# Four-bit rounding of a Perceiver block: the rounding constant made from |q| by ScalarE and a maximum by GpSimd, in place of an exponent mask on VectorE

## The reference

```
scale = max(max|xb| / 6, 1e-12)            per block of 16
q     = nearest of {0, .5, 1, 1.5, 2, 3, 4, 6} to |xb / scale|, with its sign
out   = q * scale
gate  = fq(x) @ fq(w_gate).T ;  up = fq(x) @ fq(w_up).T
y     = fq(silu(gate) * up) @ fq(w_down).T
```

## Time and profile before

| | us |
|---|---|
| median of 3 runs | 1688.79 (1688.48 to 1689.01) |
| the profiled execution, its own time | 1689.68 |
| its span in the profile | 1687.9 |
| attention stage with weight rounding | 211.8 to 347.2 |
| FP4 stage | 348.4 to 520.4 |

### The profile page before, as it was taken

The page is one execution under the profiler, slowest core; times in us unless marked ns, Lnnn a source line. Parts: engine busy times, 40 slices in busy tenths (PEclk is TensorE's granted clock), DMA queues, the critical chain, the costliest instruction groups (busy, mean ns, idle before and its releaser), DMA issues. The chain is left out here.

```text
span 1687.9 us, 26535 instructions
## 1 busy us (share of the span) xinstructions
PE 1471.6 (87%) x11120; PEld 1060.0 (63%) x11120; DVE 773.1 (46%) x1333; ACT 466.4 (28%) x772; POOL 557.9 (33%) x315
## 2 busy tenths in 40 slices
PE   8788977477988999999999999999998896936796
PEld 3556755243444778778787787788776673415573
DVE  2455279989435341332322323222232315978913
ACT  0323301031111115243242433324243431303302
POOL 6102057656323032122122122231232324617701
PEclk9779975788998999999999999999999998967997
DMA  5300030010101411111111111111012016003000
GB/s 233 149 1 1 0 137 1 0 69 0 75 0 64 147 51 57 52 34 53 39 42 51 39 48 42 38 52 57 30 42 78 22 57 256 0 0 119 1 0 25
DMA packets 50101, 91.29 MB, mean 54 GB/s; under 512 B 28600, under 2 KB 41664, under 8 KB 46912
## 3 DMA queue, kind: packets, MB, share of 16 engines
q1 hardware_dynamic: 49984, 89.60, 15.1%
HBM read 79.89 MB, written 9.70 MB: 53 GB/s over the span
## 5 line engine op out<-in xcount | busy, mean ns | idle before, releaser
L1074 POOL TENSOR_TENSOR ctx_hi<-ctx_raw,one 128x1536 fp32r<-128x1536 f32 (+1 forms) x36 | 102.9, 2858 | 617.5 <-DMA ctx_raw<-in_ctx 426.0
L1328 DVE TENSOR_TENSOR V<-PS,vbias 128x512 f32<-128x512 f32 (+1 forms) x104 | 71.9, 691 | 338.0 <-PE PS L1114 337.8
L1256 ACT COPY ET<-PS 128x512 f32<-128x512 f32 (+1 forms) x224 | 129.6, 585 | 299.1 <-PE PS L1170 295.4
L1359 DVE TENSOR_SCALAR_CACHE_REDUCE E<-PS 128x384 f32<-128x384 f32 (+1 forms) x256 | 131.8, 571 | 159.6 <-PE PS L1147 159.0
L1170 PE MATMUL PS<-ident,E 128*128 128x128 f32 (+1 forms) x832 | 127.3, 278 | 8.8 <-ACT ET L1256 8.8
L1077 POOL TENSOR_TENSOR ctx_raw_r<-ctx_raw,ctx_hi 128x1536 fp32r<-128x1536 f32 (+1 forms) x36 | 131.2, 3644 | 2.8
L1114 PE MATMUL PS<-ctx_raw_r,wk_hi 128*128 128x384 f32 (+1 forms) x512 | 128.6, 355 | 0.0
L1114 PE MATMUL PS<-wv_lo,ctx_hi 128*128 128x512 f32 (+1 forms) x416 | 125.9, 405 | 0.0
L1114 PE MATMUL PS<-ctx_hi,wk_hi 128*128 128x384 f32 (+1 forms) x512 | 122.9, 361 | 2.5 <-POOL ctx_raw_r L1077 2.5
L1263 ACT ACTIVATE E<-E,peak 128x1601 f32<-128x1601 f32 x64 | 103.5, 1623 | 64.8 <-DVE peak L1364 64.8
L1114 PE MATMUL PS<-wv_hi,ctx_hi 128*128 128x512 f32 (+1 forms) x416 | 120.5, 411 | 0.8 <-issue 0.8
(11 more groups left out here) (283 smaller groups left out, 2383.3 us busy)
## 6 DMA issues: line engine op xcount, KB each, us to landing
ctx_raw<-in_ctx SPq DMA_DIRECT2D x27, 768.0 KB, 4.4
ctx_raw<-in_ctx_first SPq DMA_DIRECT2D x9, 900.0 KB, 4.6
rel_scr<-rel_out SPq DMA_DIRECT2D x8, 640.0 KB, 3.8
fwk<-in_fwk SPq DMA_DIRECT2D x1, 4096.0 KB, 25.4
fwv<-in_fwv SPq DMA_DIRECT2D x1, 4096.0 KB, 12.7
corr<-rel_scr SPq DMA_DIRECT2D x64, 48.0 KB
p_scr<-E SPq DMA_DIRECT2D x16, 192.0 KB, 2.3
near<-p_scr SPq DMA_DIRECT2D x64, 48.0 KB
```

The lines of the kernel that those rows point to most:

```text
L1074: nc.gpsimd.tensor_tensor(ctx_hi[r][:, :, 0:n], ctx_raw[r][:, :, 0:n], one[:].unsqueeze(1).broadcast_to([P, KC, n]), ALU.mult).then_inc(S[ ...
L1256: nc.scalar.copy(ET[0:n, j % ET_RING, :], src[0:n, :]).then_inc(S["et_out"], 1)
L1328: v.tensor_tensor(V[0:rows, at % V_RING, :], bank(4 + NUMBER[unit] % 2)[0:rows, :], vbias[0:rows, :], ALU.add).then_inc(S["v_out"], 1)
L1359: v.tensor_scalar(E[:, p, k0:k0 + n], bank(r)[:, 0:n], 1.0, None, ALU.mult, ALU.max, accum_out=tops[:, p, c:c + 1]).then_inc(S["s_out"], 1)
```

## The change

The constant is made another way. With c = max((2^22 + 1)|q|, 2^22 + 1), adding and subtracting c rounds q to the same grid. ScalarE makes (2^22 + 1)|q| with one activation (`magnitude`, Abs with a scale; semaphore `scaled`), GpSimd takes the maximum with 2^22 + 1 (`tensor_scalar`) as a third operation of `round`, and L581 and L582 are gone from VectorE. For the weights, the small operations on the block maxima are done for two chunks at once (`scales` over 88 numbers instead of twice 44), there are four buffers of q and constant instead of three, six of the scales, and GpSimd joins the first 8 chunks instead of 11, VectorE the last 8. In the FP4 stage `magnitude` is put at fixed places of ScalarE's queue: behind the emptying of weight groups 2, 6, 10, 14, 18 and 21 (SIZED_AFTER), and as ("size", chunk) in ORDER; VectorE's queue keeps its order, and there are three buffers as before. `round` and `join` count three steps of `rounded` per chunk instead of two. The smallest changes of form (`scale_of`, `blocks`) are left out.

```diff
@@ small_attention, ScalarE (act)
                 if t + 1 < NT:
                     exponentials(t + 1)
+                if beside and t >= 1:
+                    beside.scalar(act, 2)
                 act.wait_ge(pt_ps, t + 1)
...
                                s.PS[:, 4:6, 0:groups * SQ].rearrange("p b (g q) -> p b g q", q=SQ)).then_inc(o_out, 1)
+                if beside:
+                    beside.scalar(act, 2)
+            if beside:
+                beside.scalar(act, 2)
@@ class Fp4
-    EXPONENT = 0x7F800000
-    MAGIC = 1.5 * 2.0 ** 22
+    GRID = 2.0 ** 22 + 1.0
...
+        self.slots = -(-(stages + 1) // together) * together
+        self.scale = region.tensor(name + "_scale", [P, self.slots, self.nb])
+        self.inverse = region.tensor(name + "_inverse", [P, together, self.nb])
...
+    def magnitude(self, act, n, width):
+
+        act.wait_ge(self.divided, n + 1)
+        self.nc.scalar.activation(self.magic[n % self.stages][:, 0:width], self.q[n % self.stages][:, 0:width], ACT.Abs,
+                                  scale=self.GRID).then_inc(self.scaled, 1)
...
+    def scales(self, dve, ch, n, xs):
+
+        nb, v, first = xs[0].shape[1], self.nc.vector, n % self.slots
+        if n + len(xs) > self.slots:
+            dve.wait_ge(self.done, n + len(xs) - self.slots)
+        for k, x in enumerate(xs):
+            ch.add(v.tensor_reduce(self.scale_of(n + k, nb), x, AX.X, ALU.max, apply_absolute_value=True))
+        ch.sync()
+        sc, inv = self.scale[:, first:first + len(xs), 0:nb], self.inverse[:, 0:len(xs), 0:nb]
+        ch.link(v.tensor_scalar(sc, sc, float(np.float32(1 / 6)), 1e-12, ALU.mult, ALU.max))
+        ch.link(v.reciprocal(inv, sc))
+        ch.link(v.tensor_scalar(inv, inv, 1.0 - 2.0 ** -23, None, ALU.mult))
+
+    def divide(self, dve, ch, n, x, k=0):
...
         if n >= self.stages:
             dve.wait_ge(self.done, n - self.stages + 1)
...
-        ch.link(v.tensor_tensor(q.rearrange("p (n j) -> p n j", j=BLOCK), x, inv.unsqueeze(2).broadcast_to([P, nb, BLOCK]), ALU.mult))
-        ch.link(v.tensor_scalar(magic.bitcast(U32), q.bitcast(U32), self.EXPONENT, None, ALU.bitwise_and))
-        v.tensor_scalar(magic, magic, 1.0, self.MAGIC, ALU.max, ALU.mult).then_inc(self.divided, 1)
+        v.tensor_tensor(blocks(self.q[r][:, 0:nb * BLOCK]), x, self.inverse[:, k, 0:nb].unsqueeze(2).broadcast_to([P, nb, BLOCK]),
+                        ALU.mult).then_inc(self.divided, 1)
@@ Fp4.round
-        pool.wait_ge(self.divided, n + 1)
+        pool.wait_ge(self.scaled, n + 1)
+        self.nc.gpsimd.tensor_scalar(magic, magic, self.GRID, None, ALU.max).then_inc(self.rounded, 1)
+        pool.wait_ge(self.rounded, 3 * n + 1)
         self.nc.gpsimd.tensor_tensor(q, q, magic, ALU.add).then_inc(self.rounded, 1)
@@ class WeightRounding
-    BY_POOL = CHUNKS - 5
+    BY_POOL = CHUNKS // 2
...
-        self.nc, self.s, self.fp4, self.started = nc, s, Fp4(nc, sem, region, "fp4w", self.WIDTH, 3), 0
+        self.nc, self.s, self.fp4, self.started = nc, s, Fp4(nc, sem, region, "fp4w", self.WIDTH, 4, 2), 0
+        self.measured = 0
...
-            self.fp4.divide(dve, ch, n, self.chunk(n))
+            if n % 2 == 0:
+                self.fp4.scales(dve, ch, n, [self.chunk(n), self.chunk(n + 1)])
+            self.fp4.divide(dve, ch, n, self.chunk(n), n % 2)
...
+    def scalar(self, act, count):
+
+        for n in range(self.measured, min(self.measured + count, self.CHUNKS)):
+            self.fp4.magnitude(act, n, self.WIDTH)
+            self.measured = n + 1
@@ fp4_layer
+    ORDER = [("turn", X0), ("gu", 0), ("turn", X0 + 1), ("gu", 1), ("size", D0 + 2), ("turn", X0 + 2), ("gu", 2), ("size", D0 + 3),
+             ("turn", X0 + 3), ("gu", 3), ("size", H0), ("turn", D0), ("gu", 4), ("turn", D0 + 1), ("gu", 5), ("turn", D0 + 2),
+             ("gu", 6), ("size", H0 + 1), ("turn", D0 + 3), ("gu", 7), ("turn", H0), ("gu", 8), ("down", 0), ("gu", 9),
+             ("size", H0 + 2), ("turn", H0 + 1), ("gu", 10), ("down", 1), ("gu", 11), ("turn", H0 + 2), ("size", H0 + 3), ("down", 2),
+             ("turn", H0 + 3), ("down", 3)]
+    SIZED_AFTER = {2: X0, 6: X0 + 1, 10: X0 + 2, 14: X0 + 3, 18: D0, 21: D0 + 1}
...
+                fp4.scales(dve, ch, n, [x])
                 fp4.divide(dve, ch, n, x)
...
-            empty(range(WEIGHTS))
+            for k in range(WEIGHTS):
+                empty([k])
+                if k in SIZED_AFTER:
+                    fp4.magnitude(act, SIZED_AFTER[k], width(SIZED_AFTER[k]))
             for kind, k in ORDER:
+                if kind == "size":
+                    fp4.magnitude(act, k, width(k))
```

More of the change, by code:

```diff
@@ L549, with __init__, scale_of @@
 class Fp4:
-    EXPONENT = 0x7F800000
-    MAGIC = 1.5 * 2.0 ** 22
-    def __init__(self, nc, sem, region, name, width, stages):
-        self.nc, self.stages = nc, stages
+    GRID = 2.0 ** 22 + 1.0
+    def __init__(self, nc, sem, region, name, width, stages, together=1):
+        self.nc, self.stages, self.together, self.nb = nc, stages, together, width // BLOCK
         tensors = lambda of, dt, w: [region.tensor(f"{name}_{of}{r}", [P, w], dt) for r in range(stages)]
         self.q, self.magic = tensors("q", F32, width), tensors("magic", F32, width)
-        self.scale, self.inverse = tensors("scale", F32, width // BLOCK), region.tensor(name + "_inverse", [P, width // BLOCK])
-        self.divided, self.rounded, self.done = (sem(name + "_" + n) for n in ("divided", "rounded", "done"))
-    def divide(self, dve, ch, n, x):
+        self.slots = -(-(stages + 1) // together) * together
+        self.scale = region.tensor(name + "_scale", [P, self.slots, self.nb])
+        self.inverse = region.tensor(name + "_inverse", [P, together, self.nb])
+        self.divided, self.scaled, self.rounded, self.done = (sem(name + "_" + n) for n in ("divided", "scaled", "rounded", "done"))
+    def magnitude(self, act, n, width):
+        act.wait_ge(self.divided, n + 1)
+        self.nc.scalar.activation(self.magic[n % self.stages][:, 0:width], self.q[n % self.stages][:, 0:width], ACT.Abs,
+                                  scale=self.GRID).then_inc(self.scaled, 1)
+    def scale_of(self, n, nb):
+        return self.scale[:, n % self.slots, 0:nb]
+    def scales(self, dve, ch, n, xs):
[10 more added lines that the diff above has]
+    def divide(self, dve, ch, n, x, k=0):
         nb, r, v = x.shape[1], n % self.stages, self.nc.vector
@@ L573, in divide @@
             dve.wait_ge(self.done, n - self.stages + 1)
[L574 to L579, removed]
[L580 to L582 removed]
+        v.tensor_tensor(blocks(self.q[r][:, 0:nb * BLOCK]), x, self.inverse[:, k, 0:nb].unsqueeze(2).broadcast_to([P, nb, BLOCK]),
+                        ALU.mult).then_inc(self.divided, 1)
     def round(self, pool, n, width):
         q, magic = self.q[n % self.stages][:, 0:width], self.magic[n % self.stages][:, 0:width]
[L587 removed]
+        pool.wait_ge(self.scaled, n + 1)
+        self.nc.gpsimd.tensor_scalar(magic, magic, self.GRID, None, ALU.max).then_inc(self.rounded, 1)
+        pool.wait_ge(self.rounded, 3 * n + 1)
         self.nc.gpsimd.tensor_tensor(q, q, magic, ALU.add).then_inc(self.rounded, 1)
[L589 removed]
+        pool.wait_ge(self.rounded, 3 * n + 2)
         self.nc.gpsimd.tensor_tensor(q, q, magic, ALU.subtract).then_inc(self.rounded, 1)
@@ L594, in join @@
         nb, r = x.shape[1], n % self.stages
-        eng.wait_ge(self.rounded, 2 * n + 2)
-        ops.tensor_tensor(x, self.q[r][:, 0:nb * BLOCK].rearrange("p (n j) -> p n j", j=BLOCK),
-                                     self.scale[r][:, 0:nb].unsqueeze(2).broadcast_to([P, nb, BLOCK]), ALU.mult).then_inc(self.done, 1)
+        eng.wait_ge(self.rounded, 3 * n + 3)
+        ops.tensor_tensor(x, blocks(self.q[r][:, 0:nb * BLOCK]),
+                          self.scale_of(n, nb).unsqueeze(2).broadcast_to([P, nb, BLOCK]), ALU.mult).then_inc(self.done, 1)
 def blocks(ap):
@@ L798, in _ @@
                     linear_to_tokens(nc, bank(4 + k % 2), s.XT, t, wuT, a, b).then_inc(u_ps, 1)
-                else:
+                elif kind == "down":
                     pe.wait_ge(turned_out, ends[H0 + k])
```

4 lines of the change are left out of this document (removed).

## The result

| us | median | lowest to highest | runs |
|---|---|---|---|
| before | 1688.9 | 1688.48 to 1689.2 | 4 |
| changed | 1713.56 | 1710.07 to 1717.32 | 4 |

The ratio is 1.0147 (95%: 1.0123 to 1.017): 24.7 us slower. The forecast was 1693.3 and the range ended at 1706, so only the direction was right. The profiled execution took 1715.18, its span is 1713.4.

A forecast was written before the change was run, and what follows sets the result against it. VectorE and GpSimd block each other in the attention stage, which GpSimd's queue ends; in the FP4 stage VectorE, later TensorE, sets the pace. Attention -6.6 and FP4 +11.1 gave +4.5: 1693.3 us, range 1680 to 1706.

The forecast's parts named there:

- Prices: Costs of moved operations; GpSimd's one-input maximum taken at 0.93 us for 704 columns, between 0.60 and 1.67.
- Attention stage: GpSimd becomes the always busy engine; its last subtraction ends at 333.5 against 340.08, -6.6 us.
- Start: Attention stage: GpSimd waits for ScalarE's first constant and begins at 234.7 instead of 231.14, 3.5 late.
- Work: Attention stage: GpSimd's 16 chunks of maximum, addition and subtraction at 4.51 each, 72.2 us; eight joins, 11.8.
- Port: Attention stage: 20 of 24 VectorE multiplications and joins each cost busy GpSimd 0.74, together 14.8 us.
- Gaps: Attention stage: three gaps of 0.08 us between GpSimd's operations in each of 16 chunks.
- FP4 stage: ScalarE's queue holds the x copy for D0+1's constant; piece 0 at 379.2 instead of 365.31, stage +11.1 us.
- The order of the chain: FP4 stage before piece 0: X0+2 joined at 365.9, D0+1 divided by 377.0, constant 1.4, x copy 0.8.
- The tail: FP4 stage's end: H0+3 is rounded with TensorE waiting, +1.3 us.
- (b): Rival for both stages: the maximum costs as much as an addition, some +18, at most +22.4, 1707 us; chance 0.14.
- (a): Rival: port doesn't hold up D0+1's constant in the FP4 stage, piece 0 at 372.7, 1677.6 us; chance 0.24.
- (c): Rival: gains and losses cancel within 0.2%, by 10 of 24 port hits or one fewer wait before piece 0; chance 0.12.

The follow-up runs named there:

- e5: Changed kernel with exponent mask and its successor back on VectorE, no constant by ScalarE, FP4 order of before: 1685.87 us, 0.9991 of before.
- e4: Changed kernel with the change in the attention stage alone, FP4 stage rounding as before: 1690.98 us, 1.0013 of before.
- e7: Changed kernel with GpSimd's maximum over only 300 of 704, 221 of 512, 592 of 1408 columns: 1690.15 us, 1.0005 of before.
- e1: Changed kernel without GpSimd's maximum, which then only adds and subtracts: 1673.13 us, 0.9906 of before.
- v3: Changed kernel with the maximum made by ScalarE through two more activations, FP4 stage as before: 1671.35 us, 0.9895 of before.
- e8: e1 with the constants of D0+1 and H0 moved back in ScalarE's queue, behind pieces 1 and 4: 1663.74 us, 0.9854 of before.
- e6: Changed kernel with GpSimd's multiplication by 1.0 in place of the maximum: 1715.58 us, one run.

## Why the prediction was wrong

**The step that failed** is the price in "Prices": "I take 0.93 (0.73 for 512, 1.67 for 1408): if reading is what costs, one stream costs half of two". Measured free of waiting: 1.96, 1.48 and 3.75. The argument that one stream is cheaper than two was never in the rows; the upper bound, the two-input price, came from the same argument and was no bound. The nearest rows, memset and addition, are other instructions, and nothing excluded a third one above both. The trace of before had no GpSimd operation of this form over a whole tile; its small ones (the deviations, one column) say nothing of the price per column. An upper bound by doubling the addition would have given 1693.3 + 16 x 2.4 = 1732 for the attention stage alone, and a range that held the time. Here the Trainium skill (GPSIMD Engine Reference, Engine selection) is not borne out in its "roughly line-rate" for one input: 2.54 ns a column stands against the 0.88 us that VectorE's reduction took for 704, that is 1.25 ns. Its other half, that an elementwise maximum belongs on VectorE and not on GpSimd, agrees with e5, where VectorE makes the whole constant: 134.1 us in the attention stage against e4's 139.3.

The price was not the only thing wrong. The forecast was 20.3 us too low, the price alone makes 23.4, and what follows shows the other errors.

**Attention stage** (forecast -6.6, measured +2.7). Counted from the stage's own start, GpSimd was to begin at 22.9 and end at 121.7; it began at 24.9 and ended at 130.7, 9.0 later. *Start:* +2.0, of which 1.6 are TensorE's clock in the first 32 matmuls; in e7, with 3.76 there, GpSimd starts at 22.8, as forecast. *Work:* 16 x (1.96 - 0.93) = 16.5 more. *Port:* nine of GpSimd's operations were lengthened by over 0.4, 6.1 in all instead of 14.8: 8.7 less. With VectorE at 76 of 112 us there were fewer meetings than the 20 of 24 that I took. *Gaps* between GpSimd's operations: 3.5 in all instead of 4.5. Together +8.8. The port term was wrong by itself and not only through the price: in e7 it is 11 operations and 7.5, and the stage is 12.7 shorter than before, 6.1 more than forecast. With no maximum (e1) it is 19.2 shorter.

**FP4 stage** (forecast +11.1, measured +25.1). Counted from the stage's start, pieces 0, 4 and 7 were forecast at 30.8, 69.0 and 95.4. With the price as forecast they stood at 30.4, 71.2 and 96.6 (e7), and the stage at +12.5. The order of the chain held: X0+2 joined, D0+1 divided, its multiplication behind one operation of GpSimd, the constant, the x copy. Its length came out by luck. VectorE's timeline in e7, whose FP4 stage starts at 336.02:

```profile
353.87 2.72 DVE L604 TENSOR_TENSOR fp_q<-wd,fp_inverse 128x1408 f32<-128x1408 f32 x1
356.51 0.68 DVE L622 TENSOR_TENSOR XN<-fp_q,fp_scale 128x512 f32<-128x512 f32 x1
...
358.75 0.20 DVE L595 TENSOR_SCALAR fp_scale<-fp_scale 128x88 f32<-128x88 f32 x1
...
359.73 0.21 DVE L597 TENSOR_SCALAR fp_inverse<-fp_inverse 128x88 f32<-128x88 f32 x1
359.98 4.52 DVE L604 TENSOR_TENSOR fp_q<-wd,fp_inverse 128x1408 f32<-128x1408 f32 x1
```

The forecast let X0+2 be joined 17.5 into the stage, as soon as GpSimd had rounded it. The division of D0 stands ahead of this join in VectorE's queue, and the join ends at 21.2, 3.7 later. On the other hand the two small operations of D0+1, for which 3.4 of waiting were counted, ran free: GpSimd had stood idle until the constant of D0 came, and then made its cut maximum (358.09 to 359.78), beside which the first of the two took its plain 0.20. From the join to the end of the multiplication it is 7.3 where 11.1 was forecast, 3.8 less.

In the changed kernel the join ends at 21.7:

```profile
367.31 1.76 DVE L621 TENSOR_TENSOR XN<-fp_q,fp_scale 128x512 f32<-128x512 f32 x1
```

and behind it the maximum of D0 now fills GpSimd's time: all three of VectorE's operations wait, and from the join to the end of the multiplication it is 12.8 instead of 7.3. With the 0.5 at the join that makes the 6.0 between the two kernels' piece 0. The three x chunks did not cost more than forecast, 4.4 each: the maximum was dearer, but the 0.9 of port waits a chunk was hardly needed. From piece 0 to piece 4 it is 43.2, where 38.2 was forecast and e7 has 40.8; the divisions of D0+3 and of H0 take 1.8 more each than in e7, and piece 0 1.3 less. *The tail:* TensorE waited 3.30 for H0+3 before:

```profile
502.52 2.69 PE L783 MATMUL PS<-ident,h 128*128 128x128 f32 x11 [3.30 <-DVE h L596]
```

and 6.70 now, 3.4 longer; 1.3 was forecast, and 1.3 + 2.1 for the dearer maximum is 3.4. The 22 matmuls behind this pause then took 12.56 instead of 11.16, the other 1.4 of the 4.8 behind piece 11.

**The rivals.** (b), that the maximum costs as much as an addition, was the right case and still too mild: it put the sum at +18 to +22. (a) fell: the multiplication of D0+1 had the wait of one operation of GpSimd, and piece 0 came after 377 even with the price as forecast (348.4 + 30.4 = 378.8). (c) fell with the price, but its first condition came true: it had 10 of 24 multiplications hit the port, 7.4 less, and measured were nine lengthened operations in the changed kernel and 11 in e7. e7, at 1.0005, is (c) with the price as forecast.

**Open.** With the code of before in it, the FP4 stage took 174.2 to 174.3 in e4, e5 and v3, against 172.3 in before. Most of it is TensorE's clock at one place. Piece 5, behind the same wait of 2.74, before:

```profile
418.57 2.82 PE L128 MATMUL PS<-wgT,XT 128*128 128x384 f32 x8 [2.74 <-DVE h L737]
```

and in e4:

```profile
417.47 4.51 PE L128 MATMUL PS<-wgT,XT 128*128 128x384 f32 x8 [2.74 <-DVE h L822]
```

at a granted clock of 1.00 and of 0.62. That is 1.7 of the 2.0; why the clock differed is not shown. So differences of 2 us between FP4 stages are not read here, and against 174.3 the changed stage is 23.1 longer, not 25.1. A version with v3's constants and e8's places in both stages was not tried.

## What to carry to other kernels

An operation that the trace doesn't hold is priced by the form of the instruction on that engine, not by the streams that it reads; while it has no row, its upper bound is well above the nearest dearer row, and measuring it alone comes before the sum. When work is moved off a full engine, look for the one that will be full next and give it nothing: with all else alike the maximum on ScalarE made a kernel 19.6 us faster than the maximum on GpSimd (v3 and e4). In an in-order queue an early small step that waits for far work holds all that stands behind it: two such places cost 9.4 us here without the maximum, and with it, mending only the first lost half of what it had won by the second. A sum that comes out right is no proof of its terms: piece 0 of e7 came within 0.4 us of the forecast by an error of 3.7 and one of 3.8 that cancel.

## What had not been expected of the hardware

- GpSimd's operation on one tile and a number (float, 128 partitions) takes 1.48 us for 512 columns, 1.96 for 704 and 3.75 for 1408, the multiplication within 0.01 us of the maximum (e6). Its addition of two tiles takes 1.27, 1.67 and 3.16, and its memset has 0.85 ns a column.
- This form can hold VectorE off nearly to its end: a small operation of VectorE that takes 0.20 alone took 3.35 beside a maximum of 1408 columns. But it often does not. Seven multiplications of 704 columns that began 0.06 to 0.07 behind a maximum took 1.45 where 0.89 is plain, and were through 0.4 to 0.5 before it; and of 11 small operations that began inside a maximum five took their plain 0.18 to 0.21. None did of the 12 that began inside a two-tile operation there, nor of the 39 in the same two stages of the kernel before. What decides it was not tested. VectorE's row and GpSimd's:

```profile
248.38 1.45 DVE L604 TENSOR_TENSOR fp4w_q<-wg,fp4w_inverse 128x704 f32<-128x704 f32 x1 [1.28 <-POOL wg L621]
```

```profile
248.32 1.96 POOL L611 TENSOR_SCALAR fp4w_magic<-fp4w_magic 128x704 f32<-128x704 f32 x1
```

- Which engine waits hangs on hundredths of a microsecond: GpSimd now starts the next operation just as VectorE is let through (377.23 and 377.25), and VectorE's 1.63 became 4.61.
